# Two attention stages: extra TensorE products with unread results behind the first projections and the first unit's score products

## The chip, the core and the metric

The kernel runs on one core of a Trainium2 chip. A core has a matrix engine (TensorE, PE in the profile), a vector engine (VectorE, DVE), an activation engine (ScalarE, ACT), GpSimd (POOL) and queues that start DMA transfers (SP). PE reads operands from the on-chip memory SBUF and writes its results into PSUM, which has eight banks of 512 fp32 columns on 128 partitions. The metric is the device time of one execution in microseconds; lower is better.

## The reference

The input x is 4 sequences of 1024 tokens, 128 wide. Four stages follow, each added to x:

```python
x = x + attention_a(layernorm(x))      # 16 heads of width 8, rotary, no mask
x = x + local_layers(layernorm(x))     # 6 layers: local attention (window 32) and a gated ffn
x = x + attention_c(layernorm(x))      # 16 heads of width 8, rotary, causal
x = x + latent_attention_and_moe(x)    # 4 heads, 8 experts, top 2
```

Each of the two attentions computes, for each head:

```python
q, k, v = x @ wq.T, x @ wk.T, x @ wv.T          # + bias in the first
q, k = rotary(q), rotary(k)
p = softmax(q @ k.T / sqrt(8))                  # causal mask in the second
out = (p @ v) @ wo.T
```

## The kernel before

Stages a, b, c and d follow one another. The change touches stages a and c, which are two calls of `mha_stage`: stage a without a mask, stage c causal.

An attention stage works on 4 batches, each with 8 tiles of 128 tokens, and on 16 units. A unit is 4 heads of one batch, units 0 to 3 belong to batch 0, and so on. The transposed keys `kt` and queries `q1`, `q2` of a unit lie on 128 partitions, with 32 rows for each head.

For each unit there are two passes. The first pass ("first", L471) makes the scores of 128 queries against up to 512 keys for one head, a product of 32 rows of the array; VectorE reduces each one to its maximum (L652). When the unit is through, "shift" (L661 to L668) writes the maxima into the rows of the queries, which are transposed again ("turn_q2"). The second pass ("second", L487) makes the scores again in the other orientation, ScalarE takes their exponential (L583), and "values" (L500) multiplies by v into bank 7. "finish" copies bank 7 out. The second pass of a unit overlaps the first pass of the next one.

In stage a a unit has 64 first products, all 512 columns wide. In stage c it has 48, 12 for each head: 4 plain ones of 512 columns, and two each of 512, 384, 256 and 128 columns that carry the mask and have four small bf16 products of `blocks` ahead of them (L468).

The order is written out by `mha_order`: a slot number for each step, sorted; every engine walks the same list. Within a stage it begins with the transposes of the weights, the norm of batch 0, two groups of four transposes (`turn_x`, L426) and eight projections (`project`, L435, fp32, 384 columns, two records each in the trace). Then VectorE, ScalarE and GpSimd rotate and split the heads; then come the transposes of unit 0's keys and queries (`turn_k` L442, `turn_q1` L453), then unit 0's first products. Among the latter stand the norm, transposes and projections of batch 1 and the transposes of unit 1. In stage a these come in this order: 34 first products, 4 transposes, 4, 8 transposes, 4, 8 transposes, 4, a projection and 4 transposes (behind the 46th first product), and then a projection behind the 50th, 54th, 58th and 62nd. In stage c, 4 transposes each stand behind the 18th, 22nd, 26th, 30th, 38th and 42nd, and one projection behind the 46th.

First products take the banks 0, 1, 2 in turn, everything else that PE makes takes 3 to 6, and bank 7 is for the values alone. The semaphores `filled` and `emptied` of a bank tie PE to the engine that reads it.

Of the kernel before, what the change touches and what calls it, by code (L numbers as in the profile page):

```python
# [18 lines left out]
P = 128  # L19
D = 128  # L20
BATCH, SEQ = 4, 1024
TILES = SEQ // P
NT = BATCH * TILES
BANK = 512
# [60 lines left out]
class Chip:  # L85
# [34 lines left out]
    def sb(self, scope, name, shape, dt=F32):  # L120
        return scope.enter_context(self.nc.sbuf_tensor(name, [P] + list(shape), dt))
# [181 lines left out]
def mha_stage(chip, name, w_names, biases, rot, causal, local=None):  # L303
    nc, ins, x, ident, banks = chip.nc, chip.ins, chip.x, chip.ident, chip.banks
# [17 lines left out]
    with ExitStack() as scope:  # L322
# [3 lines left out]
        q1, q2 = ([sb(f"{label}_{n}", [SEQ], F32R) for n in range(2)] for label in ("q1", "q2"))  # L326
        kt = [sb(f"kt{n}", [SEQ], F32R) for n in range(3)]
# [5 lines left out]
        w_qkv, w_out, raw = sb("w_qkv", [3 * D]), sb("w_out", [D]), sb("raw", [4, D])  # L333
# [7 lines left out]
        xnt, xnt2 = (chip.y[:, TILES * n:TILES * (n + 1), :].rearrange("p t d -> p (t d)") for n in (2, 3))  # L341
# [69 lines left out]
        def tensor_():  # L411
            e, q = nc.tensor, chip.tensor
            for step in order:
                kind, i = step[0], step[1] if len(step) > 1 else None
# [6 lines left out]
                if kind == "turn_x":  # L421
                    c = step[2]
# [5 lines left out]
                if kind == "project":  # L428
                    t = step[2]
                    at, turned = slot["turn_x", i, CHUNKS - 1]  # L430
                    q.wait_ge(emptied[at], turned)
                    at, copied = slot["weights",]
                    q.wait_ge(emptied[at], copied)
                    q.wait_ge(emptied[n], use - 1)
                    e.matmul(banks[n][:, 0:3 * D], xnt[:, P * t:P * (t + 1)], w_qkv[:, :],  # L435
                             start=True, stop=True).then_inc(filled[n], 1)
                if kind == "turn_k":
                    c = step[2]
                    q.wait_ge(sem["k_split"], i // 4 + 2)
                    q.wait_ge(emptied[n], use - 1)  # L440
                    for t in range(TPB):
                        made = e.transpose(banks[n][:, P * t:P * (t + 1)], unit(kx, i, TPB * c + t), ident[:, :])  # L442
                    made.then_inc(filled[n], 1)
                if kind in ("turn_q1", "turn_q2"):
                    c = step[2]
# [9 lines left out]
                if kind == "first":  # L455
                    t, c, head = step[2:]
                    hi = min(widths[t], BANK * (c + 1))
                    wide = hi - BANK * c
                    corner = causal and hi == widths[t]
                    for source in (("turn_k", i, c), ("turn_q1", i, t // TPB)):  # L460
                        at, turned = slot[source]
                        q.wait_ge(emptied[at], turned)
                    q.wait_ge(emptied[n], use - 1)
                    part = slice(ROWS * head, ROWS * (head + 1))
                    if corner:
                        q.wait_ge(sem["blocks_cast"], 1)
                        for m in range(4):
                            e.matmul(banks[n][:, wide - P + ROWS * m:wide], blocks[part, 0, m, :],  # L468
                                     blocks[part, 1, m, ROWS * m:P], start=m == 0, stop=False,
                                     skip_group_check=True, tile_position=(ROWS * head, 0))  # L470
                    e.matmul(banks[n][:, 0:wide], q1[i % 2][part, P * t:P * (t + 1)], kt[i % 3][part, BANK * c:hi],  # L471
                             start=not corner, stop=True, skip_group_check=corner,
                             tile_position=(ROWS * head, 0)).then_inc(filled[n], 1)
                if kind == "second":
                    c, k, g = step[2:]
                    lo = max(0, k * P - c * BANK) if causal else 0
                    rows_of = slice(ROWS * g, ROWS * (g + 1))
                    at, turned = slot["turn_q2", i, c]
                    q.wait_ge(emptied[at], turned)
                    q.wait_ge(emptied[n], use - 1)  # L480
                    if diagonal(c, k):
                        q.wait_ge(sem["blocks_cast"], 1)
                        for m in (3, 2, 1, 0):
                            e.matmul(banks[n][:, lo:lo + ROWS * (m + 1)], blocks[rows_of, 0, m, :],
                                     blocks[rows_of, 2, m, 0:ROWS * (m + 1)], start=m == 3, stop=False,
                                     skip_group_check=True, tile_position=(ROWS * g, 0))
                    e.matmul(banks[n][:, lo:BANK], kt[i % 3][rows_of, P * k:P * (k + 1)],  # L487
                             q2[i % 2][rows_of, BANK * c + lo:BANK * (c + 1)], start=not diagonal(c, k), stop=True,
                             skip_group_check=diagonal(c, k), tile_position=(ROWS * g, 0)).then_inc(filled[n], 1)
                if kind == "values":  # L490
                    c, k = step[2:]
# [4 lines left out]
                    for g in range(HEADS_PER_UNIT):  # L496
# [5 lines left out]
                                        stop=ended, skip_group_check=True, tile_position=(0, ROWS * g))  # L502
                    made.then_inc(sem["valued"], 1)
                if kind == "turn_back":
                    c = step[2]
# [6 lines left out]
                if kind == "turn_o":  # L512
                    c = step[2]
# [6 lines left out]
                if kind == "conclude":  # L520
                    c = step[2]
# [241 lines left out]

        sync_()
        tensor_()
        scalar_()
        vector_()
# [1533 lines left out]
```

## Time and profile before

| | |
|---|---|
| median of 3 runs | 5307.67 us (5293.55 to 5323.05) |
| the profiled execution | 5290.19 us, span 5288.8 us |
| PE busy | 4739.1 us, 90% |
| VectorE busy | 4452.8 us, 84% |
| ScalarE busy | 3689.8 us, 70% |
| mean granted TensorE clock | 0.949 |

The profile comes from one execution. Its own time is the 5290.19 us; the span runs from the first to the last instruction. "Busy" means that at least one instruction of the engine is under way; products of PE overlap, so a busy PE need not be at its peak. The granted clock is a share of 2.4 GHz; it has two levels, 1.00 and 0.50 (1.2 GHz), and a number between them is a mean over a stretch. Stage a lies at about 0 to 845 us of the span, stage b goes to about 3984 us, stage c to about 4650 us.

### The profile page before, as it was taken

What the parts mean: (1) busy time and instruction counts of PE and PEld (TensorE: products, weight loads), DVE (VectorE), ACT (ScalarE), POOL (GpSimd) and SP (SyncE); (2) the same over time, 40 slices, a digit from 0 to 9 for tenths busy, and PEclk for the clock granted to TensorE, in tenths of its full rate; (3) what the DMA queues carried; (4) which work ended last, traced back from release to release, by engine and by line L of the source; (5) the groups of instructions that cost most, each with busy time, mean ns of one, the idle gap of its engine ahead of it and who ended that gap; (6) DMA issues with size and microseconds to landing.
All of it is one profiled execution on the core that took longest, in us unless ns stands there. A gap on an engine that the chain in (4) does not pass through costs nothing. (4 is left out here: it accounts for less than half of the span.)

```text
span 5288.8 us, 145626 instructions
## 1 busy us (share of the span) xinstructions
PE 4739.1 (90%) x60536; PEld 3208.5 (61%) x60536; DVE 4452.8 (84%) x9387; ACT 3689.8 (70%) x6571; POOL 2927.2 (55%) x3441
## 2 busy tenths in 40 slices
PE   6999997999899999999999899999987999968878
PEld 3333333777777777777777777777764555544445
DVE  7989996999999999889999999999976777577665
ACT  2888885777777787777777777777763677735522
POOL 2121003878887887777788878878762011024624
PEclk6999998999999999999999999999996999989989
DMA  0000100000000000000000000000000000000000
GB/s 23 1 1 1 32 5 24 26 10 11 13 26 10 11 16 26 11 8 15 26 11 8 31 10 11 13 10 10 8 19 10 2 2 2 2 16 1 1 1 16
DMA packets 51748, 63.45 MB, mean 12 GB/s; under 512 B 12820, under 2 KB 41258, under 8 KB 50322
## 3 DMA queue, kind: packets, MB, share of 16 engines
q1 hardware_dynamic: 51090, 54.14, 3.4%
q8 instruction: 478, 7.83, 0.6%
q14 instruction: 180, 1.47, 0.1%
HBM read 25.17 MB, written 4.19 MB: 6 GB/s over the span
## 5 line engine op out<-in xcount | busy, mean ns | idle before, releaser
L1548 POOL TENSOR_TENSOR x<-x,b_norm 128x512 f32<-128x512 f32 x768 | 793.8, 1054 | 389.4 <-DVE b_norm L1413 377.7
L1162 PE MATMUL psum<-b_w_vo,b_mixed 128*128 128x128 f32 x6144 | 798.0, 279 | 10.2 <-ACT b_mixed L1278 4.3
L1162 PEld LDWEIGHTS psum<-b_w_vo,b_mixed 128*128 128x128 f32 x6144 | 756.3, 194 | 68.7 <-ACT b_mixed L1278 44.1
L652 DVE TENSOR_REDUCE a_top<-psum 128x1 f32<-128x512 f32 x1024 | 637.7, 682 | 79.8 <-PE psum L471 77.5
L583 ACT ACTIVATE a_prob<-psum 128x512 f32<-128x512 f32 x1024 | 557.1, 606 | 119.6 <-PE psum L487 111.7
L1278 ACT COPY b_mixed<-psum 128x512 f32<-128x512 f32 x768 | 435.4, 594 | 248.7 <-PE psum L1147 248.6
L1233 ACT ACTIVATE b_square<-psum 128x512 f32<-128x512 f32 x768 | 462.6, 602 | 186.1 <-PE psum L1085 182.3
L1539 POOL TENSOR_TENSOR x<-x,b_cross 128x256 f32<-128x256 f32 x768 | 565.0, 736 | 14.3 <-DVE b_cross L1397 14.3
L1541 POOL TENSOR_TENSOR x<-x,b_cross 128x256 f32<-128x256 f32 x768 | 568.3, 740 | 0.0
L1405 DVE TENSOR_REDUCE b_norm<-b_square 128x8 f32<-128x512 f32 x768 | 508.2, 663 | 44.9 <-ACT b_square L1233 38.2
L1555 POOL TENSOR_TENSOR x<-x,b_stat 128x512 f32<-128x512 f32 x384 | 405.7, 1069 | 237.6 <-DVE b_stat L1442 234.1
L1393 DVE TENSOR_TENSOR x<-psum,b_table 128x512 f32<-128x512 f32 x768 | 520.0, 677 | 6.1 <-ACT b_square L1233 5.8
L1397 DVE TENSOR_TENSOR b_cross<-psum,b_table 128x512 f32<-128x512 f32 x768 | 520.5, 678 | 0.0
L652 DVE TENSOR_REDUCE c_top<-psum 128x1 f32<-128x512 f32 (+3 forms) x768 | 383.5, 551 | 138.5 <-PE psum L471 136.2
L1094 PE MATMUL psum<-ident,x 128*128 128x128 f32 x3072 | 465.7, 274 | 19.7 <-POOL x L1548 15.5
L1094 PEld LDWEIGHTS psum<-ident,x 128*128 128x128 f32 x3072 | 376.6, 142 | 112.5 <-POOL x L1548 25.8
L583 ACT ACTIVATE c_prob<-psum 128x512 f32<-128x512 f32 (+3 forms) x768 | 334.5, 502 | 145.5 <-PE psum L487 141.1
L471 PE MATMUL psum<-a_kt,a_q 32*128 32x512 f32 x1024 | 360.0, 531 | 62.7 <-DVE a_top L652 57.3
L1130 PE MATMUL psum<-b_k_t,b_q_t 64*32 64x64 f32 (+1 forms) x26368 | 312.2, 220 | 83.5 <-issue 83.5
L471 PEld LDWEIGHTS psum<-a_kt,a_q 32*128 32x128 f32 x1024 | 148.4, 194 | 390.6 <-DVE a_top L652 308.1
L1085 PE MATMUL psum<-b_w_qk_high,b_xst_high 128*128 128x512 f32 x768 | 361.4, 471 | 7.0 <-issue 4.2
L1130 PEld LDWEIGHTS psum<-b_k_t,b_q_t 64*32 64x32 f32 x26368 | 298.1, 105 | 103.7 <-issue 91.1
(334 smaller groups left out, 11262.5 us busy)
## 6 DMA issues: line engine op xcount, KB each, us to landing
b_prev<-b_xs_x SPq DMA_DIRECT2D x24, 384.0 KB, 3.4
ab<-in_L_ffn_Wqkv SPq DMA_DIRECT2D x6, 1024.0 KB, 5.1
b_shifted_x<-y SPq DMA_DIRECT2D x24, 224.0 KB, 2.6
b_shifted_f<-y SPq DMA_DIRECT2D x48, 112.0 KB, 2.1
ab<-in_L_ffn_Wqkv SPq DMA_DIRECT2D x6, 512.0 KB, 6.5
ab<-in_L_ffn_Wo SPq DMA_DIRECT2D x6, 512.0 KB, 7.7
b_prev<-b_xs_x SPq DMA_DIRECT2D x24, 112.0 KB, 3.4
x<-in_L_attn_x SPq DMA_DIRECT2D x4, 512.0 KB, 7.6
```

The lines of the kernel that those rows point to most:

```text
L471: e.matmul(banks[n][:, 0:wide], q1[i % 2][part, P * t:P * (t + 1)], kt[i % 3][part, BANK * c:hi], start=not corner, stop=True, skip_group_ ...
L583: e.activation(prob[j % PROBS][:, lo:BANK], banks[n][:, lo:BANK], ACT.Exp, scale=scale).then_inc(emptied[n], 1)
L652: e.tensor_reduce(top2[i % 2][:, t, c, head:head + 1], banks[n][:, 0:wide], AX.X, ALU.max).then_inc(emptied[n], 1)
L1094: made = e.transpose(banks[n][:, P * p:P * (p + 1)], r[:, P * p:P * (p + 1)], ident[:, :])
L1130: made = e.matmul(heads[rows, p, to, :], qt[half, p, rows], k[:, lo:lo + wide].rearrange("p (s q) -> p s q", q=WINDOW), start=False, stop= ...
L1162: made = e.matmul(banks[n][:, 0:D], mixed[:, h, :], w_vo[l % 2][:, h, :], start=h == 0, stop=h == 2 * PAIRS - 1)
L1393: e.tensor_tensor(by_head(rot[r % ROTS]), by_head(banks[n]), bcast(table[:, t, k, :], 1, HPC), ALU.mult).then_inc(*chain.step())
L1397: e.tensor_tensor(by_head(cross[(nth[step] - 1) % 3]), by_head(banks[n]), bcast(table[:, t, k + 1, :], 1, HPC), ALU.mult).then_inc(emptied ...
L1405: e.tensor_reduce(norm[i % 2][:, 0, HPC * c:HPC * (c + 1)], by_head(square[r % 2]), AX.X, ALU.add).then_inc(sem["summed"], 1)
L1539: e.tensor_tensor(rh[:, :, 0:half], rh[:, :, 0:half], xh[:, :, half:LDIM], ALU.subtract).then_inc(*chain.step())
L1541: e.tensor_tensor(rh[:, :, half:LDIM], rh[:, :, half:LDIM], xh[:, :, 0:half], ALU.add).then_inc(sem["roped"], 1)
L1548: e.tensor_tensor(rh, rh, bcast(norm[i % 2][:, 1, HPC * c:HPC * (c + 1)], 2, LDIM), ALU.mult).then_inc(sem["scaled"], 1)
```

## The change

Two groups of products are added to PE's list; nothing is removed. Behind the last projection of batch 0 stand 16 more of the same shape (128 rows, 384 columns, fp32) that write bank 7. Behind every first product of unit 0 stand two products that use all 128 rows of the same columns of `q1` and `kt`, as wide as the first product itself; they write bank 7 too. No semaphore is raised by them, they wait for none, and nothing reads their results: bank 7 is started afresh by the first values product. This holds for both stages, so there are 32 more projection products and (64 + 48) x 2 = 224 more full-height score products in all.

```diff
@@ -434,6 +434,9 @@
                     e.matmul(banks[n][:, 0:3 * D], xnt[:, P * t:P * (t + 1)], w_qkv[:, :],
                              start=True, stop=True).then_inc(filled[n], 1)
+                    if i == 0 and t == TILES - 1:
+                        for _ in range(2 * TILES):
+                            e.matmul(banks[7][:, 0:3 * D], xnt[:, 0:P], w_qkv[:, :], start=True, stop=True)
                 if kind == "turn_k":
@@ -471,6 +474,10 @@
                     e.matmul(banks[n][:, 0:wide], q1[i % 2][part, P * t:P * (t + 1)], kt[i % 3][part, BANK * c:hi],
                              start=not corner, stop=True, skip_group_check=corner,
                              tile_position=(ROWS * head, 0)).then_inc(filled[n], 1)
+                    if i == 0:
+                        for _ in range(2):
+                            e.matmul(banks[7][:, 0:wide], q1[0][:, P * t:P * (t + 1)], kt[0][:, BANK * c:hi],
+                                     start=True, stop=True, skip_group_check=True)
```

## Rows read from the trace of the kernel before

**Rows 1.** The page: engines over the span, and the granted clock in 40 slices.
```profile
PE 4739.1 (90%) x60536; PEld 3208.5 (61%) x60536; DVE 4452.8 (84%) x9387; ACT 3689.8 (70%) x6571; POOL 2927.2 (55%) x3441
PEclk6999998999999999999999999999996999989989
```

**Rows 2.** Windows: stretch, its length, busy us of PE, PEld, DVE, ACT, POOL (instructions), clock, DMA.
```profile
32.00:34.00 2.00, 0.00 (x0) 0.00 (x0) 1.93 (x5) 0.00 (x0) 0.00 (x0) 0.80 0.00 0
118.00:142.00 24.00, 22.94 (x98) 7.30 (x98) 15.48 (x26) 13.91 (x26) 21.61 (x12) 0.50 0.00 1
4022.00:4024.00 2.00, 2.00 (x28) 1.84 (x26) 2.00 (x6) 0.00 (x0) 0.00 (x0) 0.84 0.00 0
```

**Rows 3.** Windows, DVE's first-pass reductions (L652) alone: busy us, count, clock.
```profile
46.00:105.00 59.00, 39.32 (x64) 0.50 0.00 0
105.00:118.00 13.00, 7.34 (x12) 0.50 0.00 1
118.00:142.40 24.40, 15.88 (x27) 0.50 0.00 1
142.40:187.00 44.60, 40.08 (x65) 1.00 0.00 1
4020.00:4058.00 38.00, 24.03 (x48) 0.54 0.01 1
4058.00:4081.00 23.00, 9.59 (x20) 0.50 0.00 1
4200.00:4500.00 300.00, 201.51 (x405) 0.98 0.01 2
```

**Rows 4.** PE's timeline: start, length, line, tiles, shape, count, idle before and its releaser.
```profile
20.32 8.40 PE L435 MATMUL psum<-a_w_qkv,y 128*128 128x384 f32 x16 [0.67 <-ACT y L550]
42.04 1.97 PE L442 MATMUL psum<-ident,a_kx 128*128 128x128 f32 x8 [13.32 <-ACT a_kx L542]
46.43 0.79 PE L471 MATMUL psum<-a_kt,a_q 32*128 32x512 f32 x3
...
4016.44 1.97 PE L442 MATMUL psum<-ident,c_kx 128*128 128x128 f32 x8 [10.46 <-ACT c_kx L542]
4018.20 1.90 PE L453 MATMUL psum<-ident,c_qx 128*128 128x128 f32 x8
```

**Rows 5.** DVE's timeline at the end of stage a's first unit.
```profile
104.91 0.22 DVE L661 TENSOR_REDUCE a_top<-a_top 128x32 f32<-128x64 f32 x1
```

**Rows 6.** PE's timeline at changes of shape, clock 0.50.
```profile
86.27 1.06 PE L453 MATMUL psum<-ident,a_qx 128*128 128x128 f32 x4
87.26 0.80 PE L471 MATMUL psum<-a_kt,a_q 32*128 32x512 f32 x3
...
96.58 0.79 PE L471 MATMUL psum<-a_kt,a_q 32*128 32x512 f32 x1 [0.78 <-DVE a_top L652]
97.30 1.65 PE L435 MATMUL psum<-a_w_qkv,y 128*128 128x384 f32 x2
...
2246.60 0.80 PE L1085 MATMUL psum<-b_w_qk_high,b_xst_high 128*128 128x512 f32 x1
2247.20 0.63 PE L1085 MATMUL psum<-b_w_qk_low,b_xst_high 128*128 128x512 f32 x1
...
4032.15 0.44 PE L468 MATMUL psum<-c_blocks 32*128 32x128 bf16 x4 [0.75 <-DVE c_top L652]
4032.44 0.45 PE L471 MATMUL psum<-c_kt,c_q 32*128 32x128 f32 x1
```

**Rows 7.** The same at 1.00.
```profile
142.47 0.50 PE L487 MATMUL psum<-a_q,a_kt 32*128 32x512 f32 x2
142.90 1.06 PE L500 MATMUL psum<-a_prob,a_v 128*32 128x512 f32 x8
...
915.69 0.50 PE L1085 MATMUL psum<-b_w_qk_high,b_xst_high 128*128 128x512 f32 x1
916.03 0.39 PE L1085 MATMUL psum<-b_w_qk_low,b_xst_high 128*128 128x512 f32 x1
```

## The prediction

> **What bounds the kernel now.** I read the page first, then the busy time and granted clock by window around the two attention stages, then TensorE's (PE's) own timeline, line by line, at the places the change touches.
>
> The page [rows 1] shows PE busy 90% and VectorE (DVE) 84% of the span; no single engine is full. The clock line has a 6 in the first of its 40 slices and another 6 at the thirtieth: the openings of the two attention stages. The windows [rows 2, 3] resolve this. In stage a the clock falls to 0.50 (1.2 GHz) within 32:34 and is there until 142 us; in stage c it is 1.00 for a moment after 4020 us, falls within 4022:4024 and is at 0.50 until 4081 us. Around these it is near 1.00 (2.4 GHz).
>
> How much does the low level cost today? The counts of first-pass reductions on DVE [rows 3] give the pace. Stage a, first unit: 64 reductions in 58.5 us (first F at 46.43 us, shift at 104.91 us, [rows 4, 5]). DVE is busy 39.3 us of that, so part is waiting for PE. Then 12 in 13 us, then 27 in 24.4 us at 0.50; right after, at 1.00, 65 in 44.6 us, or 0.69 us each. Stage c: 48 in 38.0 us, then 20 in 23 us at 0.50, against 0.74 us each in 4200:4500.
>
> So at most 24.4 - 27 x 0.69 = 5.9 us, plus about 4.8 us (12 in 13 us would be 8.2 us), is to be had behind stage a's first unit, and 23 - 20 x 0.74 = 8 us behind stage c's. That is the whole prize of a higher clock after unit 0.
>
> **The change, part by part.** Write F for a first-pass product (32 rows of the array, up to 512 columns), X for an added full-height one, T for one transpose, P for one projection (two records). PE runs its list in order; the additions wait for nothing, nobody reads them, DVE, ScalarE and DMA work is unchanged. Only PE time and the clock can move.
>
> *32 added P.* In stage a the eight real ones run 20.32 to 28.7 us; the first ones go 1.28 us apart, later ones 0.65 (the 16 records take 8.40 us, [rows 4]; the profile's 1.00 before the first change of level is not to be believed, the pace says 1.2 GHz until about 26 us). Sixteen more at 0.65 take 10.4 us, to 39.1 us; the next PE work, T of the keys, waits for ScalarE until 42.04 us. Cost nothing. In stage c they run 4006.0 to 4016.4 us, and the T start at 4016.44: nothing to 1 us if the clock rises later there. Without that idle time they would cost 10.4 us each.
>
> Do they hold the clock? In stage a PE stopped at 28.7 us and the clock fell in 32:34 [rows 2]; in stage c it stopped 10.46 us before the T, and those went at the low pace again [rows 4]. In the new stage a there are 3 idle us (39.1 to 42.04), a burst of eight T, another pause, eight T. I take it that the level falls before or soon after 42 us, so unit 0 begins at 0.50 as before. In stage c the T follow without a pause, at 1.00, but in the kernel before the clock was at 1.00 there too when the F began, and 3 us of narrow F lost it; the first X are only 128 columns wide. It falls there again.
>
> *Two X behind each F, the term that decides.* The naive cost is three equal streams. The rows say more, because PE pays for every change between a 32-row and a full-height shape. At 0.50 [rows 6]: F to a following full-height product 0.72 us (96.58 to 97.30); first full-height to the second 0.60 us (2246.60 to 2247.20), although its 512 columns alone take 0.43 at 1.2 GHz; full-height back to F: four T take 0.99 us (86.27 to 87.26) where eight in a row take 1.76 [rows 4], so some 0.11 to 0.14 us on top of the 0.42 stream, 0.56. Sum for F X X: 0.72 + 0.60 + 0.56 = 1.88 us. At 1.00 [rows 7]: 0.43 (142.47 to 142.90) + 0.34 (915.69 to 916.03) + 0.31 (a stream of 0.22, half of 0.43, and 0.09, which I choose between nothing and the 0.14 of the low level) = 1.08 us. DVE takes 0.60 us for a reduction (39.3 us for 64, [rows 3]), so at either level PE becomes the bound and DVE's work, its norm pieces too, is hidden beneath it. The lower end of the term is three streams at 1.00, 0.70 us with a little for each start, if the shapes cost nothing; PE then keeps up with DVE almost.
>
> *Does unit 0 climb back?* 118:142 shows PE 22.9 us of 24 busy at 0.50 and not rising [rows 2]; it is groups of 32-row products and groups of 128x32 ones, with a change of shape between them. F X X has such seams too. What did precede rises: sixteen T in a row (4016.44 to 4020, [rows 4]) and P in a row (to 26 us). In stage a, unit 0 has 34 F, 4 T, 4 F, then 8 T in a row, 4 F, 8 T, 4 F, P and 4 T, and P after every 4 F. I take the rise at the first of these clusters. The Trainium skill ("TensorE: Matmul & The Clock Gate", Part 4) says transposes do not raise the clock; by that rule the rise would wait for the P or not come and the sum would be the low-throughout case below. The rows disagree: only T stand before the rise at 4020 us.
>
> Stage a, unit 0: 38 x 1.88 + 12 T x 0.22 = 74.1 us, then at 1.00 26 x 1.08 + 12 T x 0.11 + 5 P x 0.65 = 32.7 us. Together 106.8 against 58.5: **+48 us**. Behind unit 0 the X end; 12 F with 3 P follow, a thin load that may lose the level again. Between 0 and -10.7 I take -5. Stage a: **+43 us**. The bounds: +73 (64 x 1.88 + 24 x 0.22 + 5 x 1.28 = 132 us, low throughout), and +6 (64 x 1.08 + 24 x 0.11 + 5 x 0.65 = 75 us, less 10.7 us, high throughout).
>
> Stage c, unit 0: 48 F with masks. A step of 128 columns less takes 0.107 us off each of the three streams (128 / 1.2 GHz). So 1.88, 1.56, 1.24, 0.92 us for 512 to 128 columns, and 0.29 more for the four block products (4032.15 to 4032.44, [rows 6]). Per head: 2 x (1.88 + 1.56 + 1.24 + 0.92) + 4 x 1.88 + 8 x 0.29 = 21.0; four heads 84.2; 24 T 5.3; one P 1.3: 90.8 us, less 2 us for four F still at 1.00 and 1 us for the faster T before. 87.8 against 38.0: **+50 us**. It has single groups of 4 T and one P, no 8 T in a row, so I expect no rise before the old one. High throughout, the same sum is 51 us: +13, less the 8 us behind.
>
> Both stages stand in the chain of the run: stage b waits for a, d for c, so the sum passes through. 43 + 50 = 93 us. The profiled execution took 5290.2 us, span 5288.8; the three runs have the median 5307.7, 0.3% more. 5307.7 + 93 = **5400 us**, +1.75%.
>
> **The rivals.**
> 1. *Stage a stays at 0.50 through unit 0.* For: 118:142, no rise in 24 us of dense work. +73 + 50 = 5431.
> 2. *Stage a is high early* (the T from 42 us on, behind 19 us of P, keep or restore it) and c is low. +6 + 50 = 5364. Against: the pauses above.
> 3. *High in both stages.* +6 + 13 - 8 - 1 = +10: 5318, no change. PE would show no pause, 64 F X X end to end. The Trainium skill (same page, the closing table) has sustained occupation hold the full rate; by it this is the outcome. 118:142 speaks against, since there occupation alone did not do it.
> 4. *The other side, faster: no price for the change of shape, at 1.00.* Then F X X is 0.70 us, nearly the pace of the 0.60 us reduction. Stage a: 64 x 0.70 + 5.9 = 51 against 58.5, -7.5, and -10.7; stage c: 29 us of reductions and norm or 35 us of products (51 less the changes of shape) against 38, -3, and -8. About -28: 5280. With the level held, the run is below today's once F X X is under some 0.98 us (on the line from +10 at 1.08 to -28 at 0.70), and 0.5% below only at 0.70; each of the pairs in [rows 6, 7] would have to be wrong.
> 5. *Stage c climbs too*, at its P or a T group: about +43 + 30 = 5380, inside the forecast.
>
> **How the numbers follow.** Forecast, with 5 in it: 0.65; rival 1: 0.15; rival 2: 0.11; rival 3: 0.06; rival 4: 0.03. The likeliest case has its own range of 5375 to 5420: a rise one cluster earlier or later is 3 to 7 us, 0 or -10.7 behind unit 0, 5% on 1.88 us. The range must take in rivals 1 and 2: 5350 to 5440, which leaves out 3 and 4. This kernel's runs spread by 0.5% (5293.6 to 5323.1 us), so I call within 0.5% no change. Slower: 0.91; same: 0.06 (rival 3); faster: 0.03.
>
> **What will show it.** Stage a: P end near 39 us, T start still at 42.0, clock 0.50 when F begin at 46; F to F 1.88 us, DVE waiting for F products; a rise near 119 us; shift at about 153 us instead of 104.9. Stage c: from its first F to its shift 88 us instead of 38. Units 1 to 15 keep 0.69 and 0.74 us per reduction. I am wrong if F X X is repeated in clearly less than 1.7 us at 0.50, or if the clock is 1.00 at the first F and stays there.

## The result and the profile after

| | before | after |
|---|---|---|
| median (range) | 5307.59 us (5293.55 to 5323.05, 4 runs) | 5403.17 us (5383.31 to 5416.40, 4 runs) |
| profiled execution, span | 5288.8 us | 5382.0 us |
| mean granted clock of that execution | 0.949 | 0.946 |

The ratio is 1.0177, interval 1.0151 to 1.0203: slower, well beyond the 0.5% that the prediction calls no change. The spans differ by 93.2 us. In the changed kernel the added projections are L439 and the added score products L479; the other lines move on: transposes of the keys L445, of the queries L456, first products L474, reduction L659, shift L668.

From the page of after, to be held against [rows 1]:

```profile
PE 4878.5 (91%) x60824; PEld 3273.3 (61%) x60824; DVE 4460.5 (83%) x9387; ACT 3689.6 (69%) x6571; POOL 2926.1 (54%) x3441
PEclk7999998999999999999999999999995999988989
```

PE has 139.4 us more busy time, its weight loads 64.8, DVE 7.7, the others nothing. PE's timeline of after at the start of stage a (columns as in [rows 4]):

```profile
20.60 6.93 PE L435 MATMUL psum<-a_w_qkv,y 128*128 128x384 f32 x16 [0.67 <-ACT y L557]
27.37 10.48 PE L439 MATMUL psum<-a_w_qkv,y 128*128 128x384 f32 x32
41.21 1.97 PE L445 MATMUL psum<-ident,a_kx 128*128 128x128 f32 x8 [3.35 <-ACT a_kx L549]
...
45.59 0.79 PE L474 MATMUL psum<-a_kt,a_q 32*128 32x512 f32 x1
46.31 1.22 PE L479 MATMUL psum<-a_kt,a_q 128*128 128x512 f32 x2
47.46 0.79 PE L474 MATMUL psum<-a_kt,a_q 32*128 32x512 f32 x1
```

The row of 46.31 holds two X. Asked from 47.15 us on, the timeline shows the second one alone:

```profile
46.90 0.63 PE L479 MATMUL psum<-a_kt,a_q 128*128 128x512 f32 x1
```

The added P fill the idle time: the keys' T, which waited 13.32 us in [rows 4], now wait 3.35 us and begin at 41.21. The first F comes at 45.59, and from then on each F stands 1.87 to 1.88 us behind the last: 0.72 us from F to the first X, 0.59 to the second X, 0.56 to the next F. The place where that ends:

```profile
117.50 1.05 PE L426 MATMUL psum<-ident,ab 128*128 128x128 f32 x4
118.34 1.05 PE L445 MATMUL psum<-ident,a_kx 128*128 128x128 f32 x4
119.32 0.50 PE L474 MATMUL psum<-a_kt,a_q 32*128 32x512 f32 x1
119.75 0.73 PE L479 MATMUL psum<-a_kt,a_q 128*128 128x512 f32 x2
120.41 0.49 PE L474 MATMUL psum<-a_kt,a_q 32*128 32x512 f32 x1
```

Eight T in a row, and behind them F X X takes 1.09 us. Windows of after (columns as in [rows 2]):

```profile
40.00:42.00 2.00, 0.79 (x4) 0.80 (x5) 1.76 (x1) 2.00 (x3) 2.00 (x2) 0.69 0.00 0
46.00:106.00 60.00, 60.00 (x97) 25.10 (x96) 27.76 (x67) 0.28 (x1) 0.00 (x0) 0.50 0.00 0
120.00:153.00 33.00, 33.00 (x103) 15.79 (x102) 18.46 (x30) 4.02 (x9) 0.00 (x0) 1.00 0.00 0
4060.00:4148.00 88.00, 87.59 (x301) 49.42 (x299) 32.79 (x85) 5.03 (x10) 0.00 (x0) 0.53 0.00 1
```

The clock falls in 40:42. PE is busy 60.00 of 60.00 us and DVE 27.76: PE sets the pace. The first-pass reductions alone (L659, columns as in [rows 3]):

```profile
45.00:153.00 108.00, 44.22 (x65) 0.66 0.00 0
153.00:165.00 12.00, 11.01 (x19) 0.94 0.01 2
165.00:181.00 16.00, 9.27 (x16) 0.51 0.00 1
4060.00:4148.00 88.00, 26.67 (x48) 0.53 0.00 1
```

And DVE's timeline where unit 0 ends, with the wait for PE in brackets:

```profile
151.59 0.69 DVE L659 TENSOR_REDUCE a_top<-psum 128x1 f32<-128x512 f32 x1 [0.40 <-PE psum L474]
152.32 0.22 DVE L668 TENSOR_REDUCE a_top<-a_top 128x32 f32<-128x64 f32 x1
```

The shift of unit 0 stands at 152.32 against 104.91 us in [rows 5]. Right behind it DVE makes 19 reductions in 12 us where it made 12 in 13 us [rows 3]: the clock is still 1.00 there. Then it is at 0.50 from 163.6 to 180.7 us. From the first shift to the second it is 49.7 us, before 55.8.

In stage c PE's timeline shows the P with almost no pause into the T, and the F begin at 1.00:

```profile
4047.56 10.48 PE L439 MATMUL psum<-c_w_qkv,y 128*128 128x384 f32 x32
4058.21 1.09 PE L445 MATMUL psum<-ident,c_kx 128*128 128x128 f32 x8 [0.17 <-ACT c_kx L549]
...
4060.81 0.30 PE L474 MATMUL psum<-c_kt,c_q 32*128 32x128 f32 x1
...
4065.06 0.80 PE L479 MATMUL psum<-c_kt,c_q 128*128 128x256 f32 x2
```

From 4065.06 us on they run at 0.50, and the shift comes at 4147.68, 86.9 us after the first F, before 37.8. The level was lost although PE had no pause before it:

```profile
4061.00:4065.00 4.00, 4.00 (x36) 3.13 (x35) 1.59 (x5) 0.04 (x1) 0.00 (x0) 1.00 0.02 4
```

The 93.2 us, from the starts of first F and shifts in the two traces:

| stretch | before | after | difference |
|---|---|---|---|
| start to first F of stage a | 46.4 | 45.6 | -0.8 |
| unit 0 of stage a | 58.5 | 106.7 | +48.2 |
| to the shift of unit 1 | 55.8 | 49.7 | -6.1 |
| to the shift of unit 15 | 645.0 | 646.6 | +1.6 |
| to the first F of stage c (stage b) | 3214.5 | 3212.2 | -2.3 |
| unit 0 of stage c | 37.8 | 86.9 | +49.1 |
| to the shift of unit 15 | 535.5 | 539.6 | +4.1 |
| rest | 695.3 | 694.7 | -0.6 |

Stage b has nothing changed in it and varies from 3202.9 to 3221.2 us over the profiles of this study, so a few microseconds there mean nothing. The -6.1 us behind unit 0 go with an earlier high level, and that needs no added product: the five profiles with F X X in stage a have 49.7 to 50.0 us for this stretch, before, p_only and t_hold 55.2 to 55.8, but x_in_c, whose stage a is the unchanged one, has 49.5. There the clock rose at 124.4 us, in the profile of before at 142.4:

```profile
46.00:49.00 3.00, 1.89 (x8) 0.76 (x6) 2.14 (x4) 0.72 (x2) 0.00 (x0) 1.00 0.01 3
125.00:154.00 29.00, 27.11 (x196) 9.93 (x196) 26.90 (x46) 24.98 (x48) 14.26 (x10) 1.00 0.01 1
```

These are windows of x_in_c. The first shows that its clock was also at 1.00 for some 3 us at the start of unit 0, where before had 0.50. So one and the same stage a varies in its level from one execution to the next, and by some 6 us with it.

### The profile page after: what moved, and what is told of

It reads as the page before. It is cut to its first block and busy times, and to the rows that moved or that the text cites. A ratio compares the mean times of both kernels' runs of the same rounds, so it can differ in the third digit from the quotient of the medians.

```text
span 5382.0 us, 146202 instructions
## 1 busy us (share of the span) xinstructions
PE 4878.5 (91%) x60824; PEld 3273.3 (61%) x60824; DVE 4460.5 (83%) x9387; ACT 3689.6 (69%) x6571; POOL 2926.1 (54%) x3441
## 5 line engine op out<-in xcount | busy, mean ns | idle before, releaser
L659 DVE TENSOR_REDUCE a_top<-psum 128x1 f32<-128x512 f32 x1024 | 642.6, 684 | 118.6 <-PE psum L474 117.0
L590 ACT ACTIVATE a_prob<-psum 128x512 f32<-128x512 f32 x1024 | 557.2, 606 | 119.2 <-PE psum L494 111.4
L659 DVE TENSOR_REDUCE c_top<-psum 128x1 f32<-128x512 f32 (+3 forms) x768 | 386.3, 552 | 187.9 <-PE psum L474 185.9
L474 PE MATMUL psum<-a_kt,a_q 32*128 32x512 f32 x1024 | 369.3, 518 | 49.8 <-DVE a_top L659 43.6
L474 PEld LDWEIGHTS psum<-a_kt,a_q 32*128 32x128 f32 x1024 | 149.9, 189 | 390.2 <-DVE a_top L659 282.8
```

What stands on the lines that cost most here:

```text
L590: e.activation(prob[j % PROBS][:, lo:BANK], banks[n][:, lo:BANK], ACT.Exp, scale=scale).then_inc(emptied[n], 1)
L659: e.tensor_reduce(top2[i % 2][:, t, c, head:head + 1], banks[n][:, 0:wide], AX.X, ALU.max).then_inc(emptied[n], 1)
```

## The experiments

Each is the kernel before with the edit shown, except x_one2, x_runs2, late and late2, whose edits are shown against the changed kernel and keep its P. Parts of an edit left out are marked by three dots. The added products' results are unread in all of them, so the outputs' computation is whole.

### One part alone

**p_only**: the first hunk of the change alone, 16 more P in either stage.

```diff
+                    if i == 0 and t == TILES - 1:
+                        for _ in range(2 * TILES):
+                            e.matmul(banks[7][:, 0:3 * D], xnt[:, 0:P], w_qkv[:, :], start=True, stop=True)
```

> Only the 32 added projections, no added score products. Theory (they fill idle time of TensorE, and the clock is at 0.50 again by the first score products): 0 us, within 0.3% of before; in stage a the last added projection ends near 38 us, the transposes of the keys start near 41 to 42 us as before, and the clock is 0.50 at the first score product. Rival A (the projections are not hidden): +10.4 us in each stage, +21 us, 0.4%. Rival B (they alone keep the clock up through unit 0): some -15 to -25 us.

Measured: 5292.39 us (12 runs) against 5304.28 (17 runs), ratio 0.9977, interval 0.9961 to 0.9993: 12 us faster, a little more than nothing. The profiled span is 5286.2 us. PE's timeline of it:

```profile
41.12 1.97 PE L445 MATMUL psum<-ident,a_kx 128*128 128x128 f32 x8 [3.35 <-ACT a_kx L545]
...
4020.67 1.10 PE L445 MATMUL psum<-ident,c_kx 128*128 128x128 f32 x8
```

The P cost nothing and don't keep the clock for stage a's F (0.50 from 40.6 us; from the first F to the last shift 759.9 us, before 759.2). In stage c the T run at 1.00: from the first P to the first F 20.6 us, before 21.9. These 1.3 us are all of the gain that the profiles place. The means of the granted clock say more: 0.949 in the median of these runs, 0.946 in those of before. The 17 runs of before lie between 5279.4 us at 0.949 and 5323.6 us at 0.942, and a line through them has 4.2 us for each 0.001; 0.003 is 13 us by it. But the longer stay at 1.00 that the profile shows, 7.4 us in stage a and 10.3 in stage c, makes only 17.7 x 0.5 / 5290 = 0.0017, and little of it is work that anything waits for. In which stretch the rest was, no profile of mine shows.

**x_in_a** and **x_in_c**: the second hunk alone, in one stage alone (x_in_c has `name == "c"`).

```diff
+                    if i == 0 and name == "a":
+                        for _ in range(2):
+                            e.matmul(banks[7][:, 0:wide], q1[0][:, P * t:P * (t + 1)], kt[0][:, BANK * c:hi],
+                                     start=True, stop=True, skip_group_check=True)
```

> The two full-height products behind each first product, in stage a only, and no added projections. Theory (1.88 us for each first product with its two at 0.50, 1.08 us at 1.00, with the rise at the first run of eight transposes or later): +43 us if the rise comes there, up to +73 us if it comes late; unit 0's shift near 153 to 178 us instead of 104.9. Stage c as before, 38 us for its unit 0. Rival (each added product costs its columns alone, 0.43 us at 0.50): 1.28 us for each, +20 to +25 us in unit 0.

> The two full-height products behind each first product, in stage c only, and no added projections. Theory: +50 us, with the 48 first products of unit 0 taking 87 to 91 us instead of 38; with x_in_a it adds up to the whole change, 93 to 96 us. Rival (the two stages or the projections interact): the two alone sum to something more than 10 us away from the whole.

Measured: x_in_a 5351.22 us, x_in_c 5349.64 us, against 5304.28; ratios 1.0098 (1.0066 to 1.0129) and 1.0092 (1.0059 to 1.0125). That is +47 and +45 us by the medians, +52 and +49 by the ratios. In the traces stage a takes 802.9 us in x_in_a (after 803.0), and stage c's unit 0 87.6 us in x_in_c (after 86.9). Each half reproduces its own part without the P; with the 12 us of p_only off, the parts make 89 us by the ratios, where the whole change has 1.77%, 94 us.

### What the price is made of

**x_one2**: one X behind each F in place of two (`range(1)`), P kept.

```diff
-                        for _ in range(2):
+                        for _ in range(1):
                             e.matmul(banks[7][:, 0:wide], q1[0][:, P * t:P * (t + 1)], kt[0][:, BANK * c:hi],
```

> The whole change with one added score product behind each first product instead of two. Theory (the first added product carries the change of shape, the second only its stream): at 0.50 a first product with one added takes about 1.45 us at 512 columns, so halving the products saves only 0.43 of the 1.28 us that two add over the 0.60 us pace. Stage a +26 to +46 us, stage c +37 us, total 5370 to 5390 us. Rival (cost in proportion to the number of products): half of +95, about 5355 us.

Measured: 5372.23 us against 5300.43, ratio 1.0147 (1.0118 to 1.0177). Half the added score products keep some four fifths of the loss. PE's timeline of it, and a window:

```profile
48.11 0.79 PE L474 MATMUL psum<-a_kt,a_q 32*128 32x512 f32 x1
48.83 0.80 PE L479 MATMUL psum<-a_kt,a_q 128*128 128x512 f32 x1
49.56 0.79 PE L474 MATMUL psum<-a_kt,a_q 32*128 32x512 f32 x1
```
```profile
48.00:151.00 103.00, 103.00 (x163) 43.85 (x162) 49.39 (x100) 5.90 (x11) 0.00 (x0) 0.50 0.00 0
```

F to X 0.72 us, X to F 0.73: the two changes together cost 0.59 us above the 0.43 that 512 columns take at 1.2 GHz, 0.29 each. The second X of the full change adds 1.875 - 1.445 = 0.43 us in all, its columns and no more. The starts share it out otherwise (0.59 us to the second X, and 0.56 in place of 0.73 back to F), so a single start-to-start time behind a change is not the price of that product. So at 0.50 F X X is three streams, 1.28 us, and two changes of shape, 0.59. At 1.00 F X X takes 1.09 us in after; a further X in a row takes 0.23 (2.11 us of eight less 0.50 of one in x_runs2 below), so three streams are 0.69 and the two changes 0.40.

That it is the shape and not the new operands that costs, stage b of before shows. Behind the products of 2246.60 and 2247.20 [rows 6], the first of which follows 32-row ones, comes

```profile
2247.62 0.63 PE L1085 MATMUL psum<-b_w_qk_high,b_xst_low 128*128 128x512 f32 x1
```

It has both operands new and stands 0.42 us behind the last, the bare columns; the one ahead of it, with one operand kept, stood at 0.60. The Trainium skill ("TensorEngine Tiling (Array Packing)", Tiling Modes, Key Properties) says that a change of the tiling mode drains TensorE; these rows agree, and put 0.29 us on it at 0.50 and 0.20 us at 1.00. In this execution the clock also stayed low through all of unit 0 and until 186.6 us: unit 0 of stage a took 104.2 us (+46), that of stage c 71.1 (+33, where the expectation had +37). In stage c the level was low through nearly all of unit 0 with one X and with two, so there the two can be compared: one X keeps two thirds of the loss (33 of 49 us). In stage a the later rise is in the number too.

**x_runs2**: the same number of X, eight in a row behind every fourth F, P kept.

```diff
-                    if i == 0:
-                        for _ in range(2):
+                    if i == 0 and number[step] % 4 == 0:
+                        for _ in range(8):
                             e.matmul(banks[7][:, 0:wide], q1[0][:, P * t:P * (t + 1)], kt[0][:, BANK * c:hi],
```

> The whole change with the same 224 added score products and 32 projections, but the score products gathered: eight behind every fourth first product instead of two behind each. Theory (the price is the change of shape, and seams are what keeps the clock low): one excursion for four first products instead of four; the long runs raise the clock within the first groups of stage a, and then four first products and eight added ones take about 3.7 us (0.92 us each) instead of 7.5 us; unit 0 of stage a some 70 us instead of 106.7, unit 0 of stage c about 42 to 50 us instead of 87. Total 5300 to 5330 us, within 0.5% of before. Rival (each added product costs its time wherever it stands): as the whole change, about 5400 us.

Measured: 5302.10 us against 5300.43, ratio 1.0003 (0.9988 to 1.0018): no difference. As many added products, and the whole change's 94 us are gone. PE's timeline of it:

```profile
54.18 0.50 PE L474 MATMUL psum<-a_kt,a_q 32*128 32x512 f32 x1 [0.78 <-DVE a_top L659]
54.61 2.11 PE L479 MATMUL psum<-a_kt,a_q 128*128 128x512 f32 x8
56.65 0.50 PE L474 MATMUL psum<-a_kt,a_q 32*128 32x512 f32 x3
57.93 0.49 PE L474 MATMUL psum<-a_kt,a_q 32*128 32x512 f32 x1 [0.78 <-DVE a_top L659]
```

Two changes for four F and eight X instead of eight, and the level rises at 53.5 us, 7 us behind the first F (it is low once more from 70.5 to 80.7 us). The period is 3.75 us for four F, 0.94 each, beside 1.09 for F X X at the same level, and with PE waiting for DVE in it (0.78 us). The row of 56.65 shows another thing that the runs give back: three F in a row take the 0.50 us of one together, as in before (46.43, 0.79 us for three [rows 4]), where in F X X each has a place of its own. So this edit takes away changes of shape, gives the F their overlap back and brings the level up, all at once; it shows that the 94 us hang on where the X stand, and not how they are split over the three. Unit 0 of stage a takes 68.5 us, that of stage c 46.0; that is 10 and 8 us lost, of which 5 and 6 come back in the units behind, where the clock is up earlier, and the rest is no more than the P gain.

### What holds and what raises the clock

**t_hold**: in place of the 16 P, 96 transposes that end at the same time; nothing behind the F.

```diff
+                    if i == 0 and t == TILES - 1:
+                        for _ in range(96):
+                            e.transpose(banks[7][:, 0:P], xn[:, 0, :], ident[:, :])
```

> The kernel before with 96 transposes behind the last projection of batch 0 in place of the 16 projections, in both stages (96 x 0.107 us = 10.2 us at 1.00); no added score products. Theory (transposes hold the clock as well as projections do): 1.00 until about 40 us in stage a and until the first score products in stage c, time as with the added projections alone, 0 to -12 us. Rival (they do not count): the clock falls near 33 us while the transposes still run, they take up to 20 us at 0.50 and delay the keys' transposes by some 5 us in each stage: +5 to +10 us.

Measured: 5297.71 us against 5304.28, ratio 0.9992 (0.9978 to 1.0005): no difference. One row of PE's timeline and windows of it:

```profile
27.16 10.64 PE L439 MATMUL psum<-ident,ab 128*128 128x128 f32 x96
```
```profile
30.00:36.00 6.00, 6.00 (x57) 6.00 (x56) 5.93 (x8) 1.05 (x1) 1.60 (x1) 1.00 0.01 3
38.00:40.00 2.00, 0.00 (x0) 0.00 (x0) 0.95 (x1) 1.01 (x2) 0.98 (x1) 1.00 0.00 0
40.00:42.00 2.00, 0.97 (x5) 0.97 (x6) 1.94 (x1) 1.92 (x3) 2.00 (x2) 0.63 0.00 0
```

Transposes alone hold 1.00 for 10.6 us; before, with PE idle there, it fell in 32:34 [rows 2]. It falls at 40.5 us, with P (p_only) at 40.6. The mean clock of these runs is 0.949 in the median too, as p_only's, and by the medians they are 7 us shorter than before's.

**t_then_x**: stage a only, no P: 32 more transposes behind the T of unit 0's queries, then F X X as in the change.

```diff
+                    if kind == "turn_q1" and i == 0 and c == CHUNKS - 1 and name == "a":
+                        for _ in range(32):
+                            e.transpose(banks[7][:, 0:P], xn[:, 0, :], ident[:, :])
...
+                    if i == 0 and name == "a":
+                        for _ in range(2):
+                            e.matmul(banks[7][:, 0:wide], q1[0][:, P * t:P * (t + 1)], kt[0][:, BANK * c:hi],
+                                     start=True, stop=True, skip_group_check=True)
```

> Stage a only, no added projections: 32 transposes with unread results behind the transposes of unit 0's queries, then the two full-height products behind each first product. Theory (transposes in a row raise the clock, and two full-height products behind each first product keep it up once it is up): TensorE is busy with the transposes for 4 to 7 us, the clock is 1.00 at the first score product and stays there through unit 0 at 1.09 us each; unit 0 takes about 75 us instead of 107, and the total is +10 to +22 us, against +52 measured for the same products without the transposes. Rival (transposes do not count for the clock): +52 and the 7 us of the transposes, about 5360 us, with the rise at a projection or later.

Measured: 5316.06 us against 5304.28, ratio 1.0028 (1.0014 to 1.0041): +12 to +15 us, where the same X without the T (x_in_a) had +52. PE's timeline and three windows:

```profile
45.56 3.66 PE L457 MATMUL psum<-ident,ab 128*128 128x128 f32 x32
49.15 0.50 PE L474 MATMUL psum<-a_kt,a_q 32*128 32x512 f32 x1
49.58 0.73 PE L479 MATMUL psum<-a_kt,a_q 128*128 128x512 f32 x2
50.24 0.50 PE L474 MATMUL psum<-a_kt,a_q 32*128 32x512 f32 x1
```
```profile
43.00:45.00 2.00, 1.48 (x8) 1.08 (x7) 1.01 (x1) 0.90 (x2) 0.00 (x0) 0.50 0.00 0
45.00:46.00 1.00, 1.00 (x10) 1.00 (x8) 0.00 (x0) 0.78 (x2) 0.00 (x0) 0.87 0.00 0
49.00:125.00 76.00, 75.75 (x230) 35.45 (x228) 49.08 (x99) 5.67 (x11) 0.00 (x0) 1.00 0.00 1
```

Only T stand before the rise at 45.3 us, but they are those of unit 0's keys and queries, which before has too: the first added T starts at 45.56. So this profile shows that the added T held the level until the first F, and not that they raised it. In x_in_c, with nothing added in stage a, the level rose at 45.9 us behind the same T and was lost at 49.3 among the F; in before it did not rise there. The times say that the added T matter beyond this one execution: all ten (5307.2 to 5327.0 us) lie below all four of x_in_a (5345.7 to 5362.8).

Then the same mixture that stayed at 0.50 for 60 us in after (46:106) stays at 1.00 for 76 us. Unit 0 takes 76.0 us; rival 2's sum for it was 75. The first F stands 2.7 us later than in before, behind the added T. For this mixture in stage a the level at its first product goes on, low until transposes come between (one profile of the high level, four of the low: after, after_again, after_third, x_in_a), and it is PE's bound at either. The narrower one of stage c lost the level after 4.3 us in after.

### The change again

**after_again** and **after_third**: the changed kernel itself, for its own spread.

```diff
+                    if i == 0 and t == TILES - 1:
+                        for _ in range(2 * TILES):
...
+                    if i == 0:
+                        for _ in range(2):
...
```

> The changed kernel once more, unaltered, for a second profile and more times: its four runs lay at 5383, 5390, 5416 and 5416 us. Theory (one form, but stage a's clock rises at the first run of eight transposes in some executions and later in others, since what moves is only when the level is granted): this profile shows the same 1.88 and 1.08 us for a first product with its two, and another moment of the rise; each cluster later costs 3 to 7 us, none at all some 25 us. Rival (the spread has another cause, the same in every kernel): the rise is at the same place and the time differs elsewhere.

> The changed kernel unaltered once more, with more times. Eight runs so far lay between 5383 and 5396 us, six of them, and at 5416 us, two of them. Theory (in some executions the clock does not rise at the first run of eight transposes of stage a but later, or the moment of the rise differs in stage c): the times fall apart in the same way, about one in four some 20 to 30 us above the others, where the kernel before has its own spread of 30 us; median 5390 to 5400 us. Rival (two stray runs of that chip): all within 15 us.

Measured: 5391.54 us, ratio 1.0165 (1.0134 to 1.0196), and 5396.15 us, ratio 1.0174 (1.0149 to 1.0199). In their traces the clock rises at 121.0 and at 138.7 us, after 119.2. Windows of after_third:

```profile
106.00:125.00 19.00, 19.00 (x39) 9.60 (x39) 5.85 (x9) 1.76 (x3) 0.00 (x0) 0.50 0.00 1
125.00:138.00 13.00, 13.00 (x28) 6.68 (x28) 3.83 (x6) 1.17 (x2) 0.00 (x0) 0.50 0.00 0
139.00:161.00 22.00, 22.00 (x62) 9.99 (x62) 12.28 (x18) 2.48 (x5) 0.00 (x0) 1.00 0.00 0
```

Here the level did not rise at either group of eight T (118.27 and 127.47 us), but at the P and four T that begin at 136.67 us; stage a took 809.4 us, 6.4 more. So the cluster at which it rises differs from one execution to the next (x_in_a rises at 119.8 us). Of the 13 runs of this kernel three are at 5416 to 5419 us, with mean clocks of 0.938 to 0.941, the others have 0.943 to 0.947. That is more time at the low level; where it lies stays open, as no profile is of such a run.

### Putting the products where the clock is worth something

**filled2**: X in runs of five (three where F is narrow) behind every fourth F of unit 0, pairs in unit 1, six ahead of batch 1's T, and 20 + 2 P in stage a.

```diff
...
+                    count = 0
+                    if i == 0 and number[step] % 4 == 0:
+                        count = 5 if wide == BANK else 3
+                    if i == 1 and number[step] % 4 == 0 and t < 2:
+                        count = 2
+                    for _ in range(count):
+                        e.matmul(banks[7], q1[i][:, P * t:P * (t + 1)], kt[i][:, 0:BANK],
+                                 start=True, stop=True, skip_group_check=True)
```

> A version meant to hold the clock without making TensorE the bound. In unit 0 a run of five (stage c: three behind narrow ones) full-height products of 512 columns behind every fourth first product, two behind every fourth of the first products of unit 1 up to its second tile, six at the norm of batch 1, 20 projections instead of 16 and two more between the transposes of keys and of queries in stage a; 16 in stage c. Theory (runs hold the clock at 1.00 and stay beneath VectorE's 2.4 us for four reductions): unit 0 of stage a 50 to 55 us instead of 58.5, its second pass opens at 1.00 (-10), stage c -5 to -10: in all -15 to -30 us, 5278 to 5293 us. Rival (the level is lost anyway at the pauses, or PE becomes the bound): 0 to +15 us.

Measured: 5286.23 us against 5300.43, ratio 0.9978 (0.9961 to 0.9994), no better than p_only alone. The total lies in the expected range, but its reason does not hold: unit 0 of stage a was to take 50 to 55 us and takes 62.6, before 58.5. It begins at 46.5 us, and the clock is 1.00 until 60.1, from 67.0 to 73.8 and from 90.9 on, some 39 of its 62.6 us. The runs of X take more than the level gives back.

**late** and **late2**: the P, nothing in unit 0 but 14 X behind its last F, then two X behind every fourth F of the next 12; late2 goes on with two behind every second F up to the 20th. The diff is late2's, against the changed kernel, in place of its two X; late lacks the condition from 12 to 20.

```diff
+                    last = number[end_of_first[0]]
+                    behind = number[step] - last
+                    count = 14 if behind == 0 else 2 if 0 < behind <= 12 and behind % 4 == 0 or 12 < behind <= 20 and behind % 2 == 0 else 0
+                    for _ in range(count):
+                        e.matmul(banks[7], q1[i][:, P * t:P * (t + 1)], kt[i][:, 0:BANK],
+                                 start=True, stop=True, skip_group_check=True)
```

> The 32 added projections, no added product behind the first products of unit 0 but 14 full-height ones of 512 columns behind its last one, and two behind every fourth of the next twelve, in both stages. Theory (what a high clock is worth lies behind unit 0): the run of 14 takes 4 to 6 us and raises the clock near its end, the next first products and the opening of the second pass go at 1.00, -5 to -10 us in stage a and up to -8 in stage c; net of the run 0 to -5 us in each, so -5 to -12 us on top of what the projections alone gave, 5280 to 5290 us. Rival (the level is lost again before the second pass opens): +5 us in each stage against the projections alone, about 5300 us.

> As the version with the late run (14 full-height products behind the last first product of unit 0, two behind every fourth of the next twelve), with two more behind each pair of first products from the 13th to the 20th, that is until unit 0's first values product, in both stages. In the profile of the version without them the clock fell to 0.50 at 122 us, 4 us after the second pass opened, and came back at 143 us. Theory (the thin load before the first values product loses the level): it now holds, the stretch from unit 0's shift to unit 1's is about 50 us instead of 55 in stage a, another -3 to -5 us, 5277 to 5284 us. Rival (the extra changes of shape cost as much as they save, or the level is lost anyway): 5284 to 5290 us, the stretch still 55 us.

Measured: late 5284.64 us against 5304.28, ratio 0.9969 (0.9955 to 0.9984); late2 5287.81 against 5301.41, ratio 0.9971 (0.9956 to 0.9985). The run of X in late, and the same window of both, late first:

```profile
103.69 5.65 PE L480 MATMUL psum<-a_kt,a_q 128*128 128x512 f32 x14
```
```profile
122.00:143.00 21.00, 19.95 (x92) 5.94 (x88) 12.60 (x21) 11.86 (x23) 18.48 (x12) 0.51 0.00 0
```
```profile
122.00:143.00 21.00, 19.20 (x144) 7.01 (x136) 18.20 (x31) 18.54 (x37) 17.08 (x11) 1.00 0.01 1
```

The clock rises while the 14 X run (108.4 us, late2 106.2). In late it falls again at 122.1, once second-pass groups stand among the F, and the second shift comes 55.4 us behind the first, as before (55.8). In late2 it holds, DVE makes 31 operations instead of 21, and it is 48.8 us. Stage a is 6 us shorter than before in late2's profile. But the unchanged stage a of x_in_c came to 49.5 us for the same stretch and is 3 us shorter than before's too, so one profile of late2 doesn't show that its X made the difference. Both versions beat both kernels, but their intervals overlap that of p_only, so the times don't show either that the X add to what the P do. Nor do the profiles place late's gain: stages a and c are 7.6 us longer there than in before's, and stage b, which is unchanged, is 11.6 us shorter. late2's stretch is that of its theory, its total that of its rival.

## Why the prediction was right

- **The total.** Forecast 5400 us, slower; measured 5403.17. The sum was +93; the spans differ by 93.2 us.
- **P cost nothing.** Right for the cost: P end at 37.9 us, T wait for ScalarE until 41.2. The term was off by a gain, which p_only has at 12 us (interval 4 to 21); its profile places 1.3 us of it, in stage c, where I had allowed up to 1. The rest is open.
- **The clock falls before unit 0.** Right: 40.7 us in stage a, first F at 45.6. In stage c the first F began at 1.00 and lost it 4.3 us later (before: 3.2). In stage a it could have gone otherwise: in two profiles (t_then_x, x_in_c) the level rose at unit 0's own T, at 45.3 and 45.9 us.
- **F X X is 1.88 us at 0.50 and 1.08 at 1.00.** Measured 1.875 and 1.09, and the parts are right too. The prediction had 0.72 + 0.60 + 0.56 at 0.50, the starts are 0.72 + 0.59 + 0.56 apart; at 1.00 it had 0.43 + 0.34 + 0.31, and the second X starts 0.34 us behind the first. Where the parts fail is with another count of X: 0.72 + 0.56 gives 1.28 us for one X, measured 1.445. What the three times have above the columns is the price of the excursion as a whole, 0.59 us at 0.50 for one X and for two. The sum was sound here because its rows had two full-height products behind a 32-row one, as the change has.
- **The rise at the first eight T, near 119 us.** Right in after (119.2), after_again (121.0) and x_in_a (119.8), two clusters late in after_third (138.7), for 6.4 us more; with one X (x_one2) it did not come in unit 0 at all. So the agreement to a microsecond is partly luck. That T alone can stand before a rise is shown by 4020.0 us in before, 45.3 in t_then_x and 45.9 in x_in_c; that the T made it at this place is not shown.
- **Stage a +48 in unit 0, -5 behind it, +43.** Measured +48.2, -6.1, +43.7 with the rest of the stage. The -6.1 goes with the level behind unit 0, which the unchanged stage a reached too in one profile (49.5 us in x_in_c, 55.8 in before).
- **Stage c +50.** Measured +49.1, 86.9 us against 87.8, no early rise. Rival 5 did not happen.
- **DVE's work is hidden.** Right: PE busy 60.00 of 60.00 us, DVE 27.76.

Of the rivals, the fourth (changes of shape cost nothing) is refuted by every F to F time. The second was wrong of the change but right in its mechanism: t_then_x gave it the level it asked for and took 76.0 us in unit 0 for its 75. Its stage a came out at +14 us, not +6, mostly because 5.8 us and not 10.7 came back behind unit 0. The third asked for a rise by sustained occupation alone, and 60.00 us busy at 0.50 contradict it. That occupation holds the level once it is there agrees with t_then_x in stage a (75.75 of 76 us busy), but not with stage c of after, which lost it with PE busy for 4.00 of 4 us.

## What to carry to other kernels

What filler products cost depends on where they stand: 224 of them in pairs behind single 32-row products cost 94 us, the same number in runs of eight behind every fourth cost nothing that the times show. Count the changes of shape they bring, the overlap of neighbours that they break, and the level at which they run: in stage a the same pairs lengthened unit 0 by 48 us when it began at 0.50 and by 17.5 when it began at 1.00. Ask first where the high level would shorten a wait (here behind unit 0, some 6 us in stage a, which one of four profiles with an unchanged unit 0 had anyway). And test a sum of estimated parts with another count of them before it is used anywhere else.

## What the runs showed of the hardware

Alternating 32-row and full-height products kept PE busy for 60 us without a pause and left the clock at 0.50; the same products kept 1.00 for 76 us when it was there first. The Trainium skill ("TensorE: Matmul & The Clock Gate", Part 4) says that the full rate does not engage for transposes; here 96 in a row held 1.00 for 10.6 us, and nothing but two groups of eight stood before the rise from 0.50 at 45.3 us in t_then_x (windows 43:45 and 45:46), so for this kernel's fp32 transposes the measurement decides against the rule. The same kernel's executions differ in when the clock rises (119.2 to 138.7 us). The 17 runs of before that stand beside p_only lie along a line of 4.2 us for each 0.001 of mean clock, which takes up 78% of their variance; in the 23 beside x_one2 it is 3.9 us and 46%.
